# A graph attention layer on one core: 66 tiles of gathered node rows filled by ScalarE from a transposed table

## The chip, the cores and the metric

The kernel runs on one core of a Trainium2 chip. The metric is the device time of one execution in microseconds (us). The core has five engines with instruction queues of their own: TensorE (PE; its weight loads are shown as PEld), VectorE (DVE), ScalarE (ACT), GpSimd (POOL) and SyncE (SP), and 16 DMA engines that all of them share. A DMA that SyncE or ScalarE issues has one fixed pattern of addresses; GpSimd issues the indirect DMAs, in which each row's address comes from a list of indices.

## The reference, cut to what matters

N = 12500 nodes and E = 200000 edges, 64 features, 2 heads, all in 32-bit floats. The edges are sorted by `dst`; `src` is random.

```python
h = maximum(_layernorm(x), 0)
h_edge = ((h[src] + bond) @ W).reshape(-1, H, D)
el = einsum('ehd,hd->eh', h_edge, attn_l)
er = einsum('nhd,hd->nh', (h @ W).reshape(-1, H, D), attn_r)
s = leaky_relu(el + er[dst], 0.2)
ex = exp(s - segment_max(s, dst)[dst])
alpha = ex / segment_sum(ex, dst)[dst]
ft = segment_sum(h_edge * alpha[..., None], dst).mean(axis=1)
out = x + relu((ft - ft.mean(0)) / sqrt(ft.var(0) + eps) * gamma + beta)
```

## The kernel before, in words

The edges are cut into 49 chunks of 4096 (`NCH`), a chunk into 16 groups g of 256 edges, a group into two tiles j of 128 edges, one edge a partition. So a chunk has 32 tiles (j, g), the last chunk 27. A quarter k of a chunk is four groups, 8 tiles.

**h.** At the start VectorE and ScalarE normalise x into h (125 partitions, 100 nodes each). TensorE turns h in 13 rounds of up to four blocks (`er_table`, line 803) and ScalarE copies each round from PSUM (`evacuate`, line 667) for the node scores. Each row of h with its two source scores, 66 floats, is written to the table `h_tab` in HBM (line 482). Chunks 0 and 1 gather rows of x instead and are normalised on the fly.

**The gathers.** GpSimd fetches each tile with one indirect DMA (`gather`, line 592; issue at line 599): 128 rows of `h_tab` at the indices in `srcI`, into the buffer `gat` of the chunk (two of them, in turn). `tiles_of(c, k)` lists the tiles of a quarter. Before some gathers GpSimd waits: for VectorE to have used the buffer's quarter two chunks ago (`e_ok`), and by `keep_step_late` (line 582), from chunk 5 on, at the chunk's gather 1 for the sums of two chunks before and at its gather 17 for the turned weights of the chunk before (`p_turned`). In chunks 2 to 4 `keep_step` has such waits of its own, among them chunk 3's `p_turned` at gather 27 of chunk 4.

**SyncE's tiles.** In 21 chunks (`SP_TILES`, 6, 8, ... 46) the last tile (1, 15) isn't gathered. SyncE fetches its 128 rows one by one into `sp_tile` (`load_rows`, line 484): it loads 16 offsets into registers (line 391) and issues 16 DMAs of one row each (line 491), and so on, 64 rows a chunk. In between it loads the chunk's destination numbers (`load_dst`) and the next chunk's bond features (`load_bond`, 1024 KB). For this VectorE turned the numbers of nodes into offsets at the start (line 1207, `offs_ok`).

**A chunk's work** (`chunk(c)` on each engine). For each quarter TensorE turns the bond features into PSUM bank `pt` (`turn`, line 833) and VectorE's `make_e` (line 1047) copies the two scores of each row to `elh` (line 1055) and adds h and bond into `edge` (line 1060). In a quarter with a tile of SyncE's it does that in three pieces each. TensorE adds up the scores of a chunk in PSUM `sT_ps` (32 rows, head by group, of 256 edges): `bond_scores` from the bond features (line 851), `near_scores` for the destinations (line 871), `far_scores` from `elh` (line 879). ScalarE copies them to `s_raw` (line 730), VectorE applies the leaky relu (line 1289) and finds the segments' maxima, ScalarE makes `fexp` (line 736) and `pT` (line 740), TensorE turns `pT` into `p_m` (line 926, `p_turned`), VectorE scales the one-hot matrix (line 1342), TensorE makes the sums (line 942) and VectorE adds them to `acc`, [65, 2, 12532], at columns that are read from registers (line 1370). The nodes that are finished are turned to z in blocks of 250 (`z_block`, `z_turn`), which ScalarE keeps in the space of `acc` (`z_keep`, line 720) and VectorE puts into the statistics. After the last chunk come the batch norm, ScalarE's scaling (line 776), TensorE's turning back, and the output.

Each engine runs its queue in order, with semaphores written out by hand. VectorE's `step` waits for each operation's end before the next.

## Time and profile before

| | |
|---|---|
| runs | 1986.5, 1991.77, 1992.52 us; median 1991.77 |
| profiled execution, span from first to last instruction | 1992.0 us |
| busy share | GpSimd 74%, VectorE 55%, TensorE 48%, ScalarE 6% |
| gathers of h | 1478 |
| single-row DMAs of SyncE | 2688 |
| granted TensorE clock, mean | 0.663 |

The page names no other time of the profiled execution than its span, which lies within 0.3 us of the runs' median. A busy share is an average over the span. Register loads and the issue of DMAs on SyncE and ScalarE aren't counted as busy; GpSimd's indirect DMAs are, for as long as it makes their descriptors. "issue" as the end of an idle time says that the engine waited for nothing that the profile shows. For each line of the chain of waits the profile follows back what released it.

### The profile page before, as it was taken

How to read it: one execution, taken by the hardware profiler on the slowest of the kernel's cores; microseconds unless marked ns; L12 is line 12 of the kernel's file. 1: busy time of each engine (PE TensorE's matmuls, PEld its weight loads, DVE VectorE, ACT ScalarE, POOL GpSimd, SP SyncE). 2: the span in 40 equal slices, each digit the busy share in tenths (PEclk: the TensorE clock that was granted, in tenths of full speed). 3: DMA queues.
4: the chain of work that ended last, by engine and by line, in shares of the span. 5: the costliest groups of instructions: out<-in, count | busy, mean ns of one | idle time of the engine just before them, and what ended most of it. 6: DMA issues, size and time to landing. Idle time of an engine off the chain costs nothing.

```text
span 1992.0 us, 24940 instructions
## 1 busy us (share of the span) xinstructions
PE 958.3 (48%) x6252; PEld 731.4 (37%) x6252; DVE 1094.0 (55%) x3217; ACT 120.8 (6%) x243; POOL 1474.7 (74%) x1559
## 2 busy tenths in 40 slices
PE   2647544543554435345534453554454444544455
PEld 2525333432343324234323342343234333433345
DVE  7888545544654545446545454555465545544555
ACT  2420000000000000000000000000000000000002
POOL 7777777777777777777777777777777777777771
PEclk9867766666666666666666676667666766666677
DMA  7333222223222322232223222322322222223215
GB/s 205 93 92 93 61 71 82 61 61 92 60 61 61 91 62 61 61 92 61 60 66 85 62 61 60 92 61 61 87 65 61 60 70 83 60 61 93 60 39 135
DMA packets 75938, 149.57 MB, mean 75 GB/s; under 512 B 33559, under 2 KB 36465, under 8 KB 69265
## 3 DMA queue, kind: packets, MB, share of 16 engines
q0 software_dynamic: 49568, 52.34, 14.3%
q1 hardware_dynamic: 25106, 91.83, 13.3%
q10 hardware_dynamic: 1112, 3.73, 0.7%
q8 instruction: 52, 0.85, 0.2%
q14 instruction: 100, 0.81, 0.1%
HBM read 141.18 MB, written 6.60 MB: 74 GB/s over the span
## 4 chain that ended last, share of the span: by engine, by line
POOL 71%; issue 23%; PE 2%; DVE 2%; DMA 1%; ACT 0%; ACTq 0%; SPq 0%; DVEq 0%; POOLq 0%
POOL work L599 71%; PE p_s L821 1%; PE pt L810 0%; DMA h_tab<-acc 0%; DMA acc<-in_x 0%; DVE acc L1101 0%; DVE acc L1099 0%; POOL er_run L613 0%; PE po L942 0%; PE pt L994 0%; DVE acc L1108 0%; DMA work<-h_tab,srcI 0%; PE po L994 0%; DVE work L1085 0%; PE p_r L994 0%
## 5 line engine op out<-in xcount | busy, mean ns | idle before, releaser
L599 POOL DMA_INDIRECT work<-h_tab,srcI x1478 | 1403.9, 950 | 451.1 <-issue 451.1
L1055 DVE COPY elh<-work 128x16 f32<-128x16 f32 (+2 forms) x217 | 40.7, 196 | 761.2 <-DMA work<-h_tab,srcI 760.9
L879 PE MATMUL p_s<-ident,elh 128*32 128x128 f32 x196 | 50.6, 412 | 615.7 <-DVE elh L1055 615.7
L942 PE MATMUL po<-scaled,work 128*65 128x64 f32 x3104 | 292.5, 281 | 61.6 <-issue 58.6
L942 PEld LDWEIGHTS po<-scaled,work 128*65 128x65 f32 x3104 | 287.1, 198 | 79.5 <-issue 78.6
L879 PEld LDWEIGHTS p_s<-ident,elh 128*32 128x32 f32 x196 | 25.9, 155 | 641.4 <-DVE elh L1055 637.1
L842 PE MATMUL pt<-ident,work 128*128 128x128 f32 x784 | 187.0, 386 | 73.9 <-DVE work L1060 73.8
L851 PE MATMUL p_s<-work,wpair 128*32 128x256 f32 x784 | 183.2, 388 | 1.6 <-DVEq L1016 1.6
L1370 DVE TENSOR_TENSOR acc<-acc,po 65x64 f32 x776 | 168.5, 217 | 27.6 <-DVE acc L1370 1.4
L842 PEld LDWEIGHTS pt<-ident,work 128*128 128x128 f32 x784 | 137.8, 207 | 83.8 <-DVE work L1060 81.9
L1060 DVE TENSOR_TENSOR work<-work,pt 128x512 f32<-128x512 f32 (+2 forms) x217 | 133.1, 621 | 0.4 <-PE pt L842 0.3
L851 PEld LDWEIGHTS p_s<-work,wpair 128*32 128x32 f32 x784 | 83.7, 112 | 86.1 <-issue 13.9
L1342 DVE TENSOR_TENSOR scaled<-onehot,p_m 128x2048 f32<-128x2048 f32 x48 | 109.6, 2284 | 5.2 <-PE p_m L926 5.2
L730 ACT ACTIVATE s_raw<-p_s 32x256 f32<-32x256 f32 x49 | 18.3, 374 | 1427.1 <-PE p_s L879 1427.1
L871 PE MATMUL p_s<-ohT_i,er_st 128*32 128x256 f32 x392 | 94.3, 384 | 7.1 <-DVE er_st L1203 7.1
L793 PEld LDWEIGHTS p_q<-wz,acc 65*125 65x125 f32 x376 | 83.2, 324 | 0.2 <-issue 0.2
L793 PE MATMUL p_q<-wz,acc 65*125 65x65 f32 x376 | 82.5, 398 | 0.0
L599 POOL DMA_INDIRECT work<-in_x,srcI x64 | 63.0, 984 | 20.8 <-issue 18.9
L926 PE MATMUL p_m<-ident,pT 32*128 32x32 f32 x98 | 20.4, 300 | 95.6 <-ACT pT L740 95.6
L923 PE MATMUL p_m<-fexp,ones 1*65 1x2 f32 x98 | 18.2, 252 | 91.4 <-ACT fexp L736 91.4
L871 PEld LDWEIGHTS p_s<-ohT_i,er_st 128*32 128x32 f32 x392 | 43.5, 111 | 49.3 <-DVE er_st L1203 7.2
L1201 DVE TENSOR_TENSOR ohT_i<-ohT_i,p_m 128x1024 f32<-128x1024 int32 x49 | 59.5, 1215 | 1.9 <-DMA ohT_i<-in_dst_n 1.9
(194 smaller groups left out, 962.2 us busy)
## 6 DMA issues: line engine op xcount, KB each, us to landing
work<-in_ea_t SPq DMA_DIRECT2D x49, 1024.0 KB, 7.4
sp_tile<-h_tab SPq DMA_DIRECT2D x2688, 0.3 KB
ohT_i<-in_dst_n SPq DMA_DIRECT2D x49, 512.0 KB
work<-h_tab,srcI POOLq DMA_INDIRECT x1478, 2.4
h_tab<-acc SPq DMA_DIRECT2D x1, 2887.5 KB
work<-in_x SPq DMA_DIRECT2D x1, 2800.0 KB
out<-work SPq DMA_DIRECT2D x5, 448.0 KB
acc<-in_x ACTq DMA_DIRECT2D x3, 672.0 KB
```

Of the source, the lines that this page charges most:

```text
L599: pool.indirect_dma_start(out=row, out_offset=None, in_=x if c < RAW else h_tab, in_offset=bass.IndirectOffsetOnAxis(ap=srcI[:, c, j, g:g ...
L793: m = mm(z_bank(b)[0:NP_, c0:c0 + F1], view(acc[0:F1, hd, 0:1], [[NR, NP_]], b * ZBL + r), wz[:, hd, :], start=True, stop=True)
L842: m = nc.tensor.transpose(pt[n % 2][:, (j * 2 + i) * P:(j * 2 + i + 1) * P], bt[c % 2][:, 2 * k + i, j * P:(j + 1) * P], ident[:, :])
L851: m = mm(sT_ps, wpair[:, i, :, :].rearrange("p h g -> p (h g)"), bt[c % 2][:, i, :], start=(i == 0), stop=False, skip_group_check=True)
L871: m = mm(sT_ps, er_st[:, b, :, :].rearrange("p h g -> p (h g)"), ohT[:, b, :], start=False, stop=False, skip_group_check=True)
L879: m = mm(sT_ps[:, j * P:(j + 1) * P], elh[:, c % 2, j, :, :].rearrange("p h g -> p (h g)"), ident[:, :], start=False, stop=True, skip_grou ...
L942: m = mm(bank[0:F1, w0:w0 + H * WIN], edge[c % 2][:, j, g, :], scaled[:, j * CG + g, :, :].rearrange("p h w -> p (h w)"), start=(j == 0), ...
L1055: copied = v.tensor_copy(elh[:, q, js, :, g0:g1], rows_h[:, :, :, F:FH].rearrange("p j g h -> p j h g"))
L1060: added = v.tensor_tensor(edge[q][:, js, g0:g1, 0:F], rows_h[:, :, :, 0:F], turned[:, js, g0 - GQ * k:g1 - GQ * k, :], ALU.add)
L1201: also(v.tensor_tensor(ohT, ohT_i[:, :, :], view(tgt[:, c * NB4:(c + 1) * NB4], [[1, NB4], [0, GROUP]]), ALU.is_equal))
L1342: v.tensor_tensor(scaled[:, :, :, :], view(onehot[:, :, :], [[WIN, CT], [0, H], [1, WIN]]), view(p_m[:, 0:H * CT], [[1, CT], [CT, H], [0, ...
L1370: added = v.tensor_tensor(at, at, bank[0:F1, w0:w0 + H * WIN].rearrange("p (h w) -> p h w", h=H), ALU.add)
```

## The change

1. **66 tiles are filled by ScalarE.** `col_tiles(c)`: from chunk 5 on the tile (0, 12), in even chunks (1, 12) too. `tiles_of` leaves them out, in all 66 gathers that GpSimd doesn't issue. In their place in `gat` zeros are written once.
2. **A transposed h.** The 13 rounds of turned h, which ScalarE already copies from PSUM, are also written to a table `hT_tab` [64, 12500] in HBM by 26 DMAs. After `h_tab` is written SyncE reads it back into partitions 96 to 127 of `acc`, where both halves of `acc` had nothing after the start: 32 features in each half (`hT_cols`). The rounds are kept in four buffers instead of two. VectorE turns the node numbers into columns of that table (`coffs`, ten operations). ScalarE's first chunk waits for both.
3. **The copies.** After a chunk's `pT`, ScalarE runs `load_cols(c)`: 6 batches, each of which loads 32 column numbers into registers and copies 32 columns of 32x2 numbers into `cols`.
4. **TensorE adds them** with the identity as weights into `pt` on top of the turned bond features (`turn`, for k = 3), and with `col_w` into the scores (`bond_scores`).
5. **No single-row transfers.** SyncE's `load_rows`, `sp_tile`, `offs` are gone; `make_e` has one copy and one addition again.
6. **Scores from PSUM.** ScalarE's copy to `s_raw` is gone; VectorE multiplies `sT_ps` by 0.2 into `s_low` and takes the larger of the two.
7. **z.** As partitions 96 to 127 are taken, z blocks 0 to 44 are kept in two halves in partitions 0 to 63, and one DMA puts them together at the end (`z_packed`). Some small tiles share space, and the reserve for the descriptors of GpSimd's DMAs is set to 4096 bytes a partition (`dynamic_dma_scratch_size`).

```diff
+def col_tiles(c):
+    if c < COL_FIRST:
+        return []
+    return [(j, COL_G) for j in range(EPP if c % 2 == 0 else 1)]
...
                     if (c * CG + g) * GROUP + j * P < E
-                    and not (c in SP_TILES and (j, g) == (EPP - 1, CG - 1))]
+                    and (j, g) not in col_tiles(c)]
...
+            for n, (i0, i1) in enumerate(HT):
+                sp.wait_ge(hT_ok, n + 1)
+                for b in range(EPP):
+                    sp.dma_start(hT_tab[:, b * NH + i0 * NP_:b * NH + i1 * NP_].rearrange("f (i p) -> f i p", p=NP_),
+                                 hT(n)[b * F:(b + 1) * F, 0:i1 - i0, :]).then_inc(hT_out[n % 4], 16)
...
+            sp.wait_ge(lent_free, 1)
             sp.wait_ge(htab_in, 32)
+            sp.wait_ge(ertab_in, 48)
+            for i in range(4):
+                sp.wait_ge(hT_out[i], 32 * len(HT[i::4]))
+            for i in range(H):
+                sp.dma_start(hT_cols[:, i, :], hT_tab[i * HALF:(i + 1) * HALF, :]).then_inc(cols_table_in, 16)
             for c in range(1, NCH):
-                n, half = divmod(c - (SP_TILES[0] - SP_LEAD), SP_LEAD)
-                if 0 <= n < len(SP_TILES):
-                    sp.wait_ge(sums_made, 2 * (c - 1))
-                    load_rows(n, 2 * half)
                 load_dst(c)
                 if c + 1 < NCH:
                     load_bond(c + 1)
-                if 0 <= n < len(SP_TILES):
-                    sp.wait_ge(p_turned, c)
-                    load_rows(n, 2 * half + 1)
+            sp.wait_ge(zT_ok, Z_IN)
+            sp.dma_start(zT[F:P, 0:Z_IN, :], view(acc[0:F, 1, :], [[NP_, Z_IN], [1, NP_]])).then_inc(z_packed, 16)
...
+            def load_cols(c):
+                b0 = COL_BATCHES * (c - COL_FIRST + 2)
+                for cc, j, r0 in col_batches[b0:b0 + COL_BATCHES]:
+                    n = cols_upto(cc - 1) + j
+                    if n >= COL_BUFS:
+                        act.wait_ge(cols_read, n - COL_BUFS + 1)
+                    for i, r in enumerate(col_regs(cc, j * P + r0, j * P + r0 + COL_BATCH), r0):
+                        copied = nc.scalar.activation(view(cols[0:HALF, n % COL_BUFS, 0, i:i + 1], [[P, H]]),
+                                                      view(acc[CP:P, 0, bass.ds(r, 1)], [[NACC, H]]), ACT.Copy)
+                    copied.then_inc(cols_ok, 1)
...
-                act.wait_ge(scores_made, c + 1)
-                nc.scalar.activation(s_raw[:, :], sT_ps, ACT.Copy).then_inc(scores_ok, 1)
...
                 nc.scalar.activation(pT[:, :], sdif[:, :], ACT.Exp).then_inc(p_ok, 1)
+                if COL_FIRST - 2 <= c < NCH - 2:
+                    load_cols(c)
...
+            act.wait_ge(coffs_ok, 1)
+            act.wait_ge(cols_table_in, 32)
...
+                dve.wait_ge(scores_made, c + 1)
+                step(v.tensor_scalar(s_low[:, :], sT_ps, NEG_SLOPE, None, ALU.mult))
+                v.tensor_tensor(sL, sT_ps, s_low[:, :], ALU.max).then_inc(scores_ok, 1)
                 dve.wait_ge(scores_ok, c + 1)
-                step(v.scalar_tensor_tensor(sL, s_raw[:, :], NEG_SLOPE, s_raw[:, :], ALU.mult, ALU.max))
...
-    nc = _bacc.Bacc("TRN2", target_bir_lowering=False, num_devices=1)
+    nc = _bacc.Bacc("TRN2", target_bir_lowering=False, num_devices=1, dynamic_dma_scratch_size=4096)
```

How the instructions stand in the queues, at three places. Each row is a line of the kernel, an operation, what it writes and reads, and what it waits for.

ScalarE before, from the middle of one chunk into the next (`s_raw` are the copied scores, `acc` from `p_q` a kept z block):

```order
L736 ACTIVATE fexp<-fdif 1x2 [waits open_all,open_diff]
L740 ACTIVATE pT<-sdif 32x256 [waits p_turned,diff_ok]
L730 ACTIVATE s_raw<-p_s 32x256 [waits scores_made]
L723 ACTIVATE acc<-p_q 128x125 [waits zT_made]
L736 ACTIVATE fexp<-fdif 1x2 [waits open_all,open_diff]
```

ScalarE now, chunk 3, the first with copies. A batch is one TENSOR_LOAD (32 registers) and 32 times the pair of ISA (the register instruction that makes the address) and ACTIVATE:

```order
L753 ACTIVATE acc<-p_q 64x125 [waits zT_made]
L753 ACTIVATE acc<-p_q 64x125
L783 ACTIVATE fexp<-fdif 1x2 [waits open_all,open_diff]
L787 ACTIVATE pT<-sdif 32x256 [waits p_turned,diff_ok]
L418 TENSOR_LOAD coffs
L767 ISA
L767 ACTIVATE cols<-acc 32x2
```

In every chunk from 3 to 46 there are now 6 such batches, 391 instructions more, between `pT` and the next chunk's z block and `fexp`; the wait for the scores is gone from this queue.

GpSimd before, its whole run of gathers of h:

```order
L613 DMA er_run<-er_tab,er_idx 16x64
L599 DMA work<-h_tab,srcI 128x66 x1478
L404 TENSOR_LOAD flag
```

and now:

```order
L636 DMA er_run<-er_tab,er_idx 16x64
L622 DMA work<-h_tab,srcI 128x66 x1433
L429 TENSOR_LOAD flag
```

There are 45 fewer, and the order is the same.

TensorE before, from a chunk's sums to the wait for the gathered rows' scores:

```order
L942 MATMUL po<-scaled,work 65x64 x15
L842 MATMUL pt<-ident,work 128x128 [waits e_ok]
L842 MATMUL pt<-ident,work 128x128 x3
L851 MATMUL p_s<-work,wpair 32x256 [waits scores_ok]
L851 MATMUL p_s<-work,wpair 32x256 x7
L871 MATMUL p_s<-ohT_i,er_st 32x256 [waits near_ok]
L871 MATMUL p_s<-ohT_i,er_st 32x256 x3
L879 MATMUL p_s<-ident,elh 32x128 [waits elh_ok]
```

and now, in the same place, ahead of an odd chunk (one tile):

```order
L1007 MATMUL po<-scaled,work 65x64 x15
L897 MATMUL pt<-ident,work 128x128 [waits cols_ok,e_ok]
L900 MATMUL pt<-ident,cols 128x32 x2
L897 MATMUL pt<-ident,work 128x128 x3
L910 MATMUL p_s<-work,wpair 32x256 [waits scores_ok]
L910 MATMUL p_s<-work,wpair 32x256 x7
L915 MATMUL p_s<-cols,col_w 32x128 x2
L936 MATMUL p_s<-ohT_i,er_st 32x256 [waits near_ok]
L936 MATMUL p_s<-ohT_i,er_st 32x256 x3
L944 MATMUL p_s<-ident,elh 32x128 [waits elh_ok]
```

Four multiplications more a tile, and a wait for the copied columns, both ahead of the wait for `elh`.

## Rows read from the trace of the kernel before

**Rows 1.** Page: busy us (share) xinstructions of each engine; chain that ended last, by engine

```profile
PE 958.3 (48%) x6252; PEld 731.4 (37%) x6252; DVE 1094.0 (55%) x3217; ACT 120.8 (6%) x243; POOL 1474.7 (74%) x1559
...
POOL 71%; issue 23%; PE 2%; DVE 2%; DMA 1%; ACT 0%; ACTq 0%; SPq 0%; DVEq 0%; POOLq 0%
```

**Rows 2.** Page, costliest groups: line engine op xcount | busy, mean ns | idle before

```profile
L599 POOL DMA_INDIRECT work<-h_tab,srcI x1478 | 1403.9, 950 | 451.1 <-issue 451.1
```

**Rows 3.** Waits of GpSimd: waited for, us in total, times, longest us

```profile
POOL work L599 <- issue: 470.0, 1540, 0.3
```

**Rows 4.** Timeline of GpSimd: start us, us, engine line op, idle before; four gathers

```profile
94.87 0.96 POOL L599 DMA_INDIRECT work<-h_tab,srcI  x1 [0.30 <-issue]
...
208.87 0.95 POOL L599 DMA_INDIRECT work<-h_tab,srcI  x1 [0.31 <-issue]
...
355.62 0.94 POOL L599 DMA_INDIRECT work<-h_tab,srcI  x1 [0.30 <-issue]
...
1948.63 0.95 POOL L599 DMA_INDIRECT work<-h_tab,srcI  x1 [0.30 <-issue]
```

**Rows 5.** Waits of VectorE and of TensorE, the longest of each

```profile
DVE elh L1055 <- DMA work<-h_tab,srcI: 760.9, 159, 12.2
...
PE p_s L879 <- DVE elh L1055: 615.7, 45, 18.1
```

**Rows 6.** Timeline of ScalarE at the start, three neighbours

```profile
41.43 0.59 ACT L673 ACTIVATE onehot<-pt 128x500 f32<-128x500 f32 x1 [2.39 <-PE pt L810]
41.91 0.21 ACT L665 ACTIVATE acc<-acc 125x24 f32<-125x24 f32 x1
42.03 1.48 ACT L678 ACTIVATE acc<-acc 125x1536 f32<-125x1536 f32 x1
```

**Rows 7.** Timeline of VectorE, eight additions to acc

```profile
319.33 1.98 DVE L1370 TENSOR_TENSOR acc<-acc,po 65x64 f32 x8
```

**Rows 8.** Timeline of SyncE's queue, two groups of 16 transfers; tile sp_tile, its issues

```profile
194.52 5.12 SPq L491 DMA_DIRECT2D sp_tile<-h_tab  x16
...
201.01 5.09 SPq L491 DMA_DIRECT2D sp_tile<-h_tab  x16
...
L491 SPq DMA_DIRECT2D sp_tile<-h_tab x2688: 224/228/329, 179.8 to 1821.3; - x192
```

**Rows 9.** Timeline of ScalarE, one chunk's two exponentials

```profile
302.58 0.20 ACT L736 ACTIVATE fexp<-fdif 1x2 f32<-1x2 f32 x1 [4.40 <-DVEq L1016]
...
304.69 0.42 ACT L740 ACTIVATE pT<-sdif 32x256 f32<-32x256 f32 x1 [1.90 <-DVE sdif L1318]
```

**Rows 10.** Timeline of TensorE, the turned weights of a chunk

```profile
348.77 0.42 PE L926 MATMUL p_m<-ident,pT 32*128 32x32 f32 x2 [1.94 <-ACT pT L740]
```

**Rows 11.** Windows (engines' busy us, clock, DMA share, GB/s); timeline of VectorE

```profile
334.00:336.00 2.00, 0.00 (x0) 0.00 (x0) 0.00 (x0) 0.00 (x0) 1.39 (x3) 0.50 0.94 377
...
339.12 0.17 DVE L1055 COPY elh<-work 128x16 f32<-128x16 f32 x1 [10.95 <-DMA work<-h_tab,srcI]
```

**Rows 12.** Windows at the start; VectorE and ScalarE there; page, DMA issues (us to landing)

```profile
40.00:60.00 20.00, 20.00 (x101) 20.00 (x101) 17.88 (x28) 9.14 (x13) 15.31 (x16) 1.00 0.12 26
...
72.00:84.00 12.00, 7.61 (x31) 4.56 (x30) 11.80 (x13) 7.07 (x2) 8.95 (x11) 0.92 0.92 293
...
84.97 0.22 DVE L1207 TENSOR_SCALAR offs<-offs 48x128 int32<-48x128 int32 x1
...
124.13 0.20 ACT L736 ACTIVATE fexp<-fdif 1x2 f32<-1x2 f32 x1 [4.41 <-DVEq L1016]
...
work<-in_ea_t SPq DMA_DIRECT2D x49, 1024.0 KB, 7.4
```

**Rows 13.** Timeline of TensorE, the turned weights of chunk 3

```profile
191.59 0.42 PE L926 MATMUL p_m<-ident,pT 32*128 32x32 f32 x2 [1.95 <-ACT pT L740]
```

**Rows 14.** Timeline of ScalarE at the end, the first of its last scalings

```profile
1974.34 3.21 ACT L776 ACTIVATE acc<-acc,col 128x250 f32<-128x250 f32 x4 [0.75 <-DVE col L1483]
```

**Rows 15.** Page, DMA issues: the gathers, median us from issue to landing

```profile
work<-h_tab,srcI POOLq DMA_INDIRECT x1478, 2.4
```

More of the change, by code:

```diff
@@ L50, with cols_upto @@
 PRE = NZ - 6
-SP_LEAD = 2
-SP_TILES = range(6, NCH - 1, SP_LEAD)
-SP_PARTS = (0, 32, 64, 96, 128)
-BATCH = 16
+NH = N // EPP
+COL_G = 12
+COL_FIRST = 5
+COL_BUFS = 4
+COL_BATCH = 32
+COL_BATCHES = 6
+def col_tiles(c):
+    if c < COL_FIRST:
+        return []
+    return [(j, COL_G) for j in range(EPP if c % 2 == 0 else 1)]
+def cols_upto(c):
+    return sum(len(col_tiles(i)) for i in range(c + 1))
 ZIN = NZ - 1
@@ L108, in gnn_kernel @@
         elh = sb("elh", [P, 2, EPP, H, CG])
-        offs = sb("offs", [P, P], i32)
-        sp_tile = sb("sp_tile", [P, 2, FH])
+        coffs, coffs_t, coffs_u = (sb(n, [P, EPP * P], i32) for n in ("coffs", "coffs_t", "coffs_u"))
+        cols = sb("cols", [P, COL_BUFS, H, P])
+        col_w = sb("col_w", [P, H, H, CG])
         raw_mv = sb("raw_mv", [P, 2, EPP, CG])
@@ L264, in gnn_kernel @@
         ertab_in = sem("ertab_in")
-        offs_in = sem("offs_in")
-        offs_ok = sem("offs_ok")
-        sp_rows_in = [sem(f"sp_rows_in{i}") for i in range(4)]
+        coffs_in = sem("coffs_in")
+        coffs_ok = sem("coffs_ok")
+        hT_out = [sem(f"hT_out{i}") for i in range(4)]
+        cols_table_in = sem("cols_table_in")
+        cols_ok = sem("cols_ok")
+        cols_read = sem("cols_read")
+        z_packed = sem("z_packed")
         er_idx_in = sem("er_idx_in")
@@ L386, in tiles_of, with col_regs @@
                     if (c * CG + g) * GROUP + j * P < E
-                    and not (c in SP_TILES and (j, g) == (EPP - 1, CG - 1))]
-        def far_regs(c, o0, o1, last, which):
+                    and (j, g) not in col_tiles(c)]
+        def col_regs(c, o0, o1):
             return nc.values_load_multi_w_load_instructions(
-                offs[c:c + 1, o0:o1], engines=[which], min_val=0, max_val=last,
+                coffs[c:c + 1, o0:o1], engines=[mybir.EngineType.Activation], min_val=0, max_val=N - 1,
                 skip_runtime_bounds_check_because="src and dst hold numbers of nodes")[1]
-        h_bytes = h_tab.rearrange("n f -> (n f)").bitcast(u8)
         def gathers_upto(c, k):
@@ L723, in z_keep, with z_keep_halves @@
                 nc.scalar.activation(zT[:, b, :], z_turned(b), ACT.Copy).then_inc(kept, 1)
+            def z_keep_halves(b):
+                act.wait_ge(zT_made, b + 1)
+                for r in range(NR):
+                    kept = nc.scalar.activation(acc[0:F, r, b * NP_:(b + 1) * NP_], z_turned(b)[r * F:(r + 1) * F], ACT.Copy)
+                kept.then_inc(zT_ok, 1)
+            col_batches = [(c, j, r0) for c in range(NCH) for j, g in col_tiles(c) for r0 in range(0, P, COL_BATCH)]
+            assert len(col_batches) <= COL_BATCHES * (NCH - COL_FIRST)
+            def load_cols(c):
[8 more added lines that the diff above has]
+                    copied.then_inc(cols_ok, 1)
             def chunk(c):
@@ L728, in chunk @@
                     z_keep(NZ - 5, zT_made, zT_ok)
[L729 to L732 removed]
+                if c == NCH - 1:
+                    z_keep(NZ - 4, zT_made, zT_ok)
+                else:
+                    for b in z_seen(c):
+                        z_keep_halves(b)
                 act.wait_ge(open_diff, c + 1)
@@ L853, in bond_scores @@
                 m.then_inc(bond_scored, 1)
+                for j, g in col_tiles(c):
+                    for i in range(H):
+                        m = mm(sT_ps[:, j * P:(j + 1) * P], col_w[0:HALF, i, :, :].rearrange("p h g -> p (h g)"),
+                               cols[0:HALF, (cols_upto(c - 1) + j) % COL_BUFS, i, :], start=False, stop=False,
+                               skip_group_check=True)
+                    m.then_inc(cols_read, 1)
             def own_turn():
@@ L1131, in _ @@
             step(v.tensor_copy(wB[:, :, :], view(wlr[0:F, :], [[1, H], [0, P]])))
+            for i in range(H):
+                step(v.tensor_copy(col_w[0:HALF, i, :, COL_G], wlr[i * HALF:(i + 1) * HALF, 0:H]))
             signal(wr_ok)
@@ L1261, in z_stat, with z_stat_halves @@
                 also(v.bn_stats(stats[:, at:at + BN6], zT[:, b, :]))
+            def z_stat_halves(b):
+                dve.wait_ge(zT_ok, b + 1)
+                at = b * BN6 + (3 if b >= PRE else 0)
+                for r in range(NR):
+                    also(v.bn_stats(stats[r * F:(r + 1) * F, at:at + BN6], acc[0:F, r, b * NP_:(b + 1) * NP_]))
             def pre_stats():
@@ L1392, in closing @@
                 v.bn_stats(stats[:, (NZ - 1) * BN6 + 3:NZ * BN6 + 3], z_turned(NZ - 1)).then_inc(last_read, 1)
+            for i in range(2):
+                dve.wait_ge(hT_out[i], 32 * len(HT[i::4]))
             for c in range(NCH - 2):
```

105 lines of the change are left out of this document (58 added, 47 removed).

## The prediction

> **What bounds the kernel now.** I read the page's busy shares first, then the chain of waits, then GpSimd's row and its waits, and then one period of the timeline engine by engine. GpSimd is busy 74% of the span, more than any other engine, and 71% of the chain that ended last is its own [rows 1]. That is its line 599, the indirect gather: 1403.9 us of work and 451.1 us of "issue" gaps for 1478 gathers, so (1403.9 + 451.1) / 1478 = 1.255 us each [rows 2]. Its waits show nothing but "issue", 0.3 us at the longest, so GpSimd never waits for a result [rows 3]; it goes on from the first gather of h (94.87 us) to the last one (1948.63 us), and a tail of 43.4 us follows [rows 4]. The others wait for it: VectorE 760.9 us for gathered rows, TensorE 615.7 us for VectorE behind them [rows 5]. So the time is the count of gathers times 1.255 us, plus start and tail, as long as no other engine needs more than a period. A period is one chunk: before, 31 gathers in the 21 chunks in which SyncE helps, 32 in the others.
>
> **What the change takes from GpSimd.** Of the 66 tiles that ScalarE now fills, 21 take the place of tiles that SyncE fetched row by row. The gathers of h fall from 1478 to 1433, and 45 x 1.255 = 56.5 us, all on the chain.
>
> **What it costs ScalarE.** This is the unknown. Between two chunks' exponentials ScalarE now runs 6 batches, each a load of 32 registers and 32 pairs of a register instruction and a copy of 32x2 numbers.
> *A pair.* From below: on ScalarE an operation with 24 elements a partition starts at 41.91 and the next at 42.03, though it takes 0.21; so 0.12 us apart; 500 elements take 0.59, that is (0.59 - 0.21) / 476 = 0.8 ns an element, so with 2 instead of 24 it would be 0.10 [rows 6]. From above: VectorE's line 1370 is such a pair, and 8 take 1.98 us, 0.25 each; but there each operation awaits the end of the one before, and the register instruction is hidden under it [rows 7]. In between: 16 of SyncE's row transfers, each behind one register move, take 5.12 us, so 0.32 each, of which the transfer's issue is 0.228; a register instruction with its gaps is worth 0.09 on a queue [rows 8]. A pair is then the longer of 0.10 (engine) and 0.09 plus a short hand-over (queue). I take 0.105 us, nearest to ScalarE's own row, and keep 0.10 and 0.25 as ends.
> *A load.* SyncE loads 16 registers between two groups of 16 transfers: 201.01 - 194.52 - 5.12 = 1.37 us [rows 8]. For 32 that is between 1.4 (all of it fixed) and 2.7 (all by the register); I take the middle, 2.1.
> *A chunk.* Six loads 12.6; 192 pairs 20.2; from the start of fexp to the end of pT 304.69 + 0.42 - 302.58 = 2.5 [rows 9]; a z block kept in two halves, twice some 0.25, 0.5. Sum 35.8 us. The period becomes 30 or 31 gathers in turn, 30.5 x 1.255 = 38.3 us. So ScalarE fits, with 2.5 us to spare; a pair of (38.3 - 12.6 - 3.0) / 192 = 0.118 us is where it no longer does.
> Queued behind the copies on ScalarE is the next chunk's fexp and pT; TensorE waits for those (p_m), VectorE's scaled one-hot for TensorE, the sums for VectorE. GpSimd, too, waits at its gather 17 for the p_m of the chunk before: turned at 348.77 + 0.42 = 349.19, reached at 355.62, 6.4 us of slack [rows 4, 10]. So a single late exponential costs nothing, only an average above the period does.
> The Trainium skill ("ScalarE: Activation LUTs", What ACT_TABLE_LOAD costs) gives an ACTIVATE with immediate operands 186 ns + 0.833 ns an element, with about 93 ns of overlap between neighbours; an estimate from it is 0.095 us a copy, and a chunk would be 33.8. The trace agrees as far as its operations go; none of its rows has a copy behind a register instruction.
>
> **SyncE** loses 2688 row transfers of 0.32 us, 20 us a chunk and more. They were hidden, but held up the loads behind them (1.5 MB a chunk), which then met the last gathers: from 334 to 336 us the DMA engines are 94% busy, and that chunk's last rows are used at 339.12 only, after 10.95 us of waiting [rows 11]. That collision goes and brings nothing, since GpSimd doesn't wait for it.
> **VectorE** loses some small copies and additions in every second chunk, and gains one operation of about 0.4 us on the scores (it reads them from PSUM where ScalarE copied them first). It is 55% busy; I cost this at nothing, under its 760.9 us of waiting [rows 1, 5]. In the last chunk that cover is gone: 0.3 us.
> **TensorE** gets four short multiplies a tile, up to 3 us a chunk, under 615.7 us of waiting in 45 places, 13.7 each [rows 5]. Nothing.
>
> **The start.** VectorE gets ten operations on 49x256 numbers ahead of chunk 0. One on 48x128 takes 0.22, so ten are about 4 us: fexp of chunk 0 moves from 124.13 to 128.5. ScalarE also has to wait there for the turned table: written in 26 pieces from 38 us on, while the DMA engines are 12% busy, and read back, 3.2 MB, after the flag at about 88. At the 293 GB/s of 72 to 84 us that takes 11 us, at the pace of a 1024 KB load in 7.4 us it takes 23: it lands at 99 to 111, ahead of 124 [rows 12]. The h table's own write (72 to 84) keeps its place before GpSimd's first gather of it. What is late next is GpSimd's gather 27 of chunk 4 at 208.87, which needs the p_m of chunk 3, turned at 191.59 + 0.42; 17 us of slack take the 4 [rows 4, 13]. Nothing.
> **The end.** One DMA of 1.4 MB packs the z blocks of all but the last chunks. It isn't wanted before ScalarE's last scaling at 1974.34, and takes 5 to 10 us at the two paces above [rows 12, 14]. Nothing.
>
> **Sum.** The profiled execution spans 1992.0 us, 0.2 above the median of the runs, 1991.8. 1991.8 - 56.5 + 0.3 = **1935.6 us**.
>
> **The rivals.** *A. ScalarE becomes the bound.* The chain then runs over its 44 stretches of copies. Each 0.01 us of a pair above 0.118 costs 192 x 0.01 x 44 = 84 us, less 6.4 of slack once. At 0.13 the period is 12.6 + 25.0 + 3.0 = 40.6: 44 x 2.3 - 7 = 94 over the forecast, **2030 us**. At the upper end, 0.25, it would be over 3000. For it: the margin is 2.5 us in 38, and no row has the pair. Against it: 0.12 with 24 elements on the engine itself. It decides from a pair of 0.118, or a load of 2.5. Chance 0.16.
> *B. A little of that:* a pair of 0.119 to 0.125 (at 0.121 the period is 38.8, 44 x 0.5 - 7 = 15 more), or the column table comes tens of us late and the first chunks with it. **1941 to 1985 us**. Chance 0.08.
> *C. Gathers get dearer.* The reserve for their descriptors is set to 4096 bytes. A gather lands 2.4 us after its issue and the next follows after 1.255, so two are under way [rows 2, 15]. If the reserve held only one, each would cost 2.4 in place of 1.255: 1433 x 1.15 = 1650 us more, **3580 us**. No row shows how many it holds. Chance 0.01.
> *D. Register loads are slow.* At 0.2 us a register a load is 6.4, a chunk 38.4 + 20.2 + 3.0 = 61.6, and the time 1935.6 + 44 x 23.3 - 7 = **2954 us**. Rows 8 speak against it, 16 registers in 1.37. Chance 0.02. The figure of 0.2 is the Trainium skill's ("Runtime: NRT & Kernel Launch", Instruction fetch mechanics); the trace doesn't agree for SyncE's loads, 0.086 at most.
> *E. No change:* a pair near 0.126 gives back what was won, 1986 to 1998. Chance 0.03.
>
> **How the numbers follow.** The forecast has 0.70. About 0.3%, 6 us, is what a measurement of this kernel can tell from no change. Faster: 0.70 + 0.08 = 0.78; within 0.3%: 0.03; slower: 0.16 + 0.01 + 0.02 = 0.19. The range takes the forecast and B, and the edge of E: 1929 (the spread of the runs, 6 us, below) to 1988. The forecast's own is 1929 to 1941.
>
> **What would show it.** Right: 1433 gathers at 1.255 us with "issue" gaps alone, the last one near 1892; 8448 copies in stretches of about 33 us, with ScalarE idle between a stretch and the next fexp; the column table landed before 120 us. Wrong: GpSimd waiting for TensorE's p_m; ScalarE without idle time in mid-kernel; periods over 38.3 us. "Issue" gaps over 0.3 us on GpSimd would speak for C.

## The result, and the profile after

The changed kernel takes 1943.2 us (median of 4 runs, 1941.2 to 1946.5) against 1992.1 for the kernel before on the same chip (4 runs, 1986.5 to 1992.9): ratio 0.9759, 95% interval 0.9744 to 0.9775, so 2.4% faster. The forecast was 1935.6, with 1929 to 1941 as its own range and 1929 to 1988 as the whole one. The sign, the mechanism and the size are right; the time came out 7.6 us above the forecast, 2 us outside its own range. The profiled execution spans 1941.6 us.

The page of the changed kernel (busy us and share; the chain that ended last; the two groups that matter, with busy us, mean ns of one and the idle time before them):

```profile
PE 1074.3 (55%) x6780; PEld 791.7 (41%) x6780; DVE 1130.0 (58%) x3242; ACT 1053.2 (54%) x8687; POOL 1426.6 (73%) x1514
...
POOL 63%; issue 22%; DVE 7%; PE 4%; DMA 1%; ACT 1%; ACTq 1%; DVEq 0%
...
L622 POOL DMA_INDIRECT work<-h_tab,srcI x1433 | 1356.3, 946 | 444.1 <-issue 436.7
L767 ACT ACTIVATE cols<-acc 32x2 f32 x8448 | 939.0, 201 | 524.8 <-issue 503.3
```

Beside [rows 1, 2] ScalarE has gone from 6% busy to 54%, and has only 1% of the chain, its queue another 1%. GpSimd has 1433 gathers instead of 1478, but its idle time is no longer all "issue": 444.1 - 436.7 = 7.4 us have another cause. Its waits, and those of the engines that feed it, name that cause (engine line waited for: us in total, times, longest):

```profile
PE p_q L845 <- ACT acc L753: 145.2, 43, 18.3
PE p_m L988 <- ACT fexp L783: 31.9, 14, 12.7
DVE scaled L1419 <- PE p_m L991: 26.5, 28, 13.8
ACT L783 <- DVEq L1081: 25.9, 1, 25.9
PE po L928 <- DMA er_run<-er_tab,er_idx: 21.8, 1, 21.8
...
POOL work L622 <- PE p_m L991: 7.4, 1, 7.4
```

GpSimd waits once, 7.4 us, for p_m, the turned weights of a chunk; before there was no such line [rows 3]. The timeline of ScalarE shows from where (start us, us, engine line op, count, idle before):

```profile
138.22 1.28 ACT L783 ACT_TABLE_LOAD   x1 [25.86 <-DVEq L1081]
139.52 0.20 ACT L783 ACTIVATE fexp<-fdif 1x2 f32<-1x2 f32 x1
...
202.81 0.20 ACT L783 ACTIVATE fexp<-fdif 1x2 f32<-1x2 f32 x1 [3.44 <-DVEq L1081]
204.92 0.41 ACT L787 ACTIVATE pT<-sdif 32x256 f32<-32x256 f32 x1 [1.91 <-DVE sdif L1395]
207.23 3.51 ACT L767 ACTIVATE cols<-acc 32x2 f32 x32 [1.90 <-issue]
212.66 2.66 ACT L767 ACTIVATE cols<-acc 32x2 f32 x24 [1.91 <-issue]
...
237.50 1.16 ACT L767 ACTIVATE cols<-acc 32x2 f32 x10 [0.18 <-issue]
238.69 0.55 ACT L753 ACTIVATE acc<-p_q 64x125 f32<-64x125 f32 x2
239.27 0.20 ACT L783 ACTIVATE fexp<-fdif 1x2 f32<-1x2 f32 x1
239.38 0.40 ACT L787 ACTIVATE pT<-sdif 32x256 f32<-32x256 f32 x1
```

and that of GpSimd:

```profile
234.69 0.95 POOL L622 DMA_INDIRECT work<-h_tab,srcI  x1 [0.31 <-issue]
243.00 0.95 POOL L622 DMA_INDIRECT work<-h_tab,srcI  x1 [7.36 <-PE p_m L991]
...
1893.53 0.95 POOL L622 DMA_INDIRECT work<-h_tab,srcI  x1 [0.31 <-issue]
```

Chunk 0's fexp comes at 139.52 instead of 124.13 [rows 12], so chunk 3's comes at 202.81; the first stretch of copies, 33.3 us long, runs from 205.3 to 238.66; chunk 4's exponentials stand behind it; and GpSimd, at gather 17 of chunk 5, has to wait for them until 243.0. After that it never waits again. The last gather starts at 1893.53, 55.1 us earlier than before [rows 4]. The tail after it is 1941.6 - 1893.5 = 48.1 us instead of 43.4. So 45 gathers and some shorter gathers won about 62 us, the one wait cost 7.1 (7.4 less the gap of 0.3), and the tail 4.7.

### The profile page after: what moved, and what is told of

Same layout as the page of the kernel before. It is cut to its first block, busy times and chain, and to the rows that moved or that the text cites. A ratio compares the mean times of both kernels' runs of the same rounds, so it can differ in the third digit from the quotient of the medians.

```text
span 1941.6 us, 37629 instructions
## 1 busy us (share of the span) xinstructions
PE 1074.3 (55%) x6780; PEld 791.7 (41%) x6780; DVE 1130.0 (58%) x3242; ACT 1053.2 (54%) x8687; POOL 1426.6 (73%) x1514
## 4 chain that ended last, share of the span: by engine, by line
POOL 63%; issue 22%; DVE 7%; PE 4%; DMA 1%; ACT 1%; ACTq 1%; DVEq 0%
POOL work L622 63%; PE p_s L873 1%; PE po L1007 1%; DMA acc<-in_x 1%; ACT cols L767 1%; ACTq L418 1%; PE pt L862 1%; DVE work L1148 0%; DVE scaled L1146 0%; DMA work<-h_tab,srcI 0%; DVE acc L1447 0%; PE p_s L910 0%; PE pt L897 0%; DVE acc L1156 0%; DVE acc L1154 0%
## 5 line engine op out<-in xcount | busy, mean ns | idle before, releaser
L622 POOL DMA_INDIRECT work<-h_tab,srcI x1433 | 1356.3, 946 | 444.1 <-issue 436.7
L767 ACT ACTIVATE cols<-acc 32x2 f32 x8448 | 939.0, 201 | 524.8 <-issue 503.3
L1108 DVE COPY elh<-work 128x16 f32<-128x16 f32 x196 | 37.7, 193 | 638.1 <-DMA work<-h_tab,srcI 636.5
L1007 PE MATMUL po<-scaled,work 128*65 128x64 f32 x3104 | 289.5, 280 | 63.9 <-issue 60.9
L1007 PEld LDWEIGHTS po<-scaled,work 128*65 128x65 f32 x3104 | 284.2, 196 | 81.7 <-issue 80.9
L944 PE MATMUL p_s<-ident,elh 128*32 128x128 f32 x196 | 49.8, 406 | 409.4 <-DVE elh L1108 409.4
L897 PE MATMUL pt<-ident,work 128*128 128x128 f32 x784 | 203.5, 393 | 60.5 <-DVE work L1112 60.0
L910 PE MATMUL p_s<-work,wpair 128*32 128x256 f32 x784 | 202.4, 417 | 1.6 <-DVEq L1081 1.6
L944 PEld LDWEIGHTS p_s<-ident,elh 128*32 128x32 f32 x196 | 25.7, 154 | 434.6 <-DVE elh L1108 430.1
L1112 DVE TENSOR_TENSOR work<-work,pt 128x512 f32<-128x512 f32 x196 | 132.9, 678 | 1.0 <-PE pt L897 0.9
L910 PEld LDWEIGHTS p_s<-work,wpair 128*32 128x32 f32 x784 | 89.9, 120 | 98.9 <-issue 34.6
L783 ACT ACTIVATE fexp<-fdif 1x2 f32<-1x2 f32 x49 | 9.9, 203 | 119.8 <-DVEq L1081 119.6
L787 ACT ACTIVATE pT<-sdif 32x256 f32<-32x256 f32 x49 | 20.3, 415 | 85.7 <-DVE sdif L1395 85.7
L1252 DVE TENSOR_TENSOR onehot<-p_m,rel_i 128x1024 f32<-128x1024 f32 x49 | 59.6, 1217 | 0.2 <-DVE coffs L1308 0.2
## 6 DMA issues: line engine op xcount, KB each, us to landing
acc<-hT_tab SPq DMA_DIRECT2D x2, 1562.5 KB, 14.2
```

What stands on the lines that cost most here:

```text
L622: pool.indirect_dma_start(out=row, out_offset=None, in_=x if c < RAW else h_tab, in_offset=bass.IndirectOffsetOnAxis(ap=srcI[:, c, j, g:g ...
L767: copied = nc.scalar.activation(view(cols[0:HALF, n % COL_BUFS, 0, i:i + 1], [[P, H]]), view(acc[CP:P, 0, bass.ds(r, 1)], [[NACC, H]]), AC ...
L897: m = nc.tensor.transpose(pt[n % 2][:, at:at + P], bt[c % 2][:, 2 * k + i, j * P:(j + 1) * P], ident[:, :])
L910: m = mm(sT_ps, wpair[:, i, :, :].rearrange("p h g -> p (h g)"), bt[c % 2][:, i, :], start=(i == 0), stop=False, skip_group_check=True)
L944: m = mm(sT_ps[:, j * P:(j + 1) * P], elh[:, c % 2, j, :, :].rearrange("p h g -> p (h g)"), ident[:, :], start=False, stop=True, skip_grou ...
L1007: m = mm(bank[0:F1, w0:w0 + H * WIN], edge[c % 2][:, j, g, :], scaled[:, j * CG + g, :, :].rearrange("p h w -> p (h w)"), start=(j == 0), ...
```

## The experiments

On two of the five visits to a chip that these runs took, the first two, the kernel before took about 2624 us instead of 1988 to 1992, and each variant that also ran on a normal visit was slower too. They are told last, because they need the others to be read. The changed kernel itself, run again as a control on a normal visit:

> The changed kernel as it is, a control. In the last two calls the kernel before took 2623 to 2625 us where it had taken 1992, and its relatives lost time to engines waiting for their next instruction. Theory A (a condition of those visits, in which instructions reach the engines slowly, and which weighs on straight-line code with very many short instructions): if the kernel before takes about 2624 here, the changed kernel takes 3040 to 3080, since late_numbers and tail_full, which are almost it, did. If before takes about 1992, this one takes 1943. Theory B (the slow times come from the edits of those kernels): the changed kernel takes less than before here too, ratio about 0.976.

It took 1938.7 us against 1988.0 (ratio 0.9751, 0.9735 to 0.9767), theory A's case. It has the same wait at the same gather (7.5 us after 233.95), the last gather at 1889.9, span 1937.7. The other kernels of normal visits are compared with this one.

**Start, stall and tail: late_both.**

```
-    if c < COL_FIRST:
+    if c < COL_FIRST or c == NCH - 1:            # no column tiles in the last chunk
...
+            sp.wait_ge(own_turned, 1)            # SyncE, ahead of the column table's load
             for i in range(H):
                 sp.dma_start(hT_cols[:, i, :], ...)
...
+                if b0 == 0:                      # ScalarE, in load_cols
+                    act.wait_ge(coffs_ok, 1)
+                    act.wait_ge(cols_table_in, 32)
...
-            act.wait_ge(coffs_ok, 1)             # ScalarE, ahead of chunk 0
-            act.wait_ge(cols_table_in, 32)
...
                 chunk(c)
+                if c == 0:                       # VectorE: the ten operations on coffs
+                    col_numbers()
```

> The changed kernel with three edits whose effects stand in different places of the trace: column numbers and ScalarE's waits moved behind chunk 0; column table loaded after er_run is turned; no column tiles in the last chunk (two gathers more, 1435). Theory: the start is back (fexp(0) at about 125 instead of 139.5), so GpSimd's one wait of 7.1 us goes; the last gather starts at 1893.5 - 7.1 + 2.5 = 1889.0 and the tail behind it is back from 48.1 to about 43.5. Time 1938.7 (the changed kernel in the last call) - 7.1 + 2.5 - 4.6 = about 1929.5. Rival 1 (the first stretch of copies makes the stall by itself): stall stays 7, time 1936.6. Rival 2 (the tail is long for a cause in the end phase): tail stays 48, time 1934. If the slow condition of the first calls is back, only the order of the traces is read.

Measured 1931.6 us (ratio 0.9712, 0.9698 to 0.9725), 7.1 us less than the changed kernel where 9.2 were expected. Its timelines of ScalarE, TensorE (start), GpSimd (last gather) and TensorE (end):

```profile
125.48 0.20 ACT L787 ACTIVATE fexp<-fdif 1x2 f32<-1x2 f32 x1 [14.09 <-DVEq L1083]
...
95.56 2.00 PE L930 MATMUL po<-ident,er_run 128*32 128x32 f32 x112 [10.21 <-DMA er_run<-er_tab,er_idx]
...
1887.17 0.94 POOL L623 DMA_INDIRECT work<-h_tab,srcI  x1 [0.30 <-issue]
...
1882.35 1.89 PE L938 MATMUL p_s<-ohT_i,er_st 128*32 128x256 f32 x8
1884.56 1.14 PE L847 MATMUL po<-wz,acc 65*125 65x65 f32 x8 [0.32 <-issue]
...
1890.21 1.06 PE L946 MATMUL p_s<-ident,elh 128*32 128x128 f32 x4 [4.39 <-DVE elh L1110]
```

Three things are to be seen. *The start:* fexp of chunk 0 is at 125.48, and the wait for p_m has gone from GpSimd's list altogether. er_run, VectorE's input for chunk 0, is turned at 95.56. In the changed kernel that row is

```profile
109.68 2.09 PE L928 MATMUL po<-ident,er_run 128*32 128x32 f32 x112 [21.78 <-DMA er_run<-er_tab,er_idx]
```

14 us later, because the seven gathers of er_run landed beside the column table's own load, whose two DMAs of 1562.5 KB were issued at 91.01 and took 14.2 us each; from 91 to 110 us the DMA engines are 96% busy, against 13% from 88 to 97 in late_both, where the table's load comes at 97.9. The other runs bear it out: the row stands at 95.8 to 96.5 in the kernel before, b_scratch, b_no_rows_2 and all_in, which have no such load there, and at 107.5 to 109.7 in the four normal executions that have it. VectorE had other work for part of that and stood for 5.9 us, until 0.1 us after TensorE had turned er_run (109.68 + 2.09 = 111.77):

```profile
103.67 2.29 DVE L1140 SCALAR_TENSOR_TENSOR work<-work,p_q 128x2048 f32<-128x2048 f32 x1
111.88 0.56 DVE L1284 COPY er_all<-po 128x384 f32<-128x384 f32 x1 [5.93 <-issue]
...
127.64 0.36 DVE L1299 TENSOR_SCALAR coffs_t<-coffs 49x256 int32<-49x256 int32 x1
...
132.07 1.23 DVE L1252 TENSOR_TENSOR onehot<-p_m,rel_i 128x1024 f32<-128x1024 f32 x1 [0.21 <-DVE coffs L1308]
```

The 15.4 us of delay are then 5.9 for er_run; 4.4 for the ten operations (127.64 to 132.07); 1.3 for the load of the Exp table, which used to lie in idle time and now stood right ahead of fexp; 3.2 by which VectorE's row at 103.67 was late already (it stood at 100.43 before, at 101.40 in late_both); and 0.6 of small shifts. Of the 3.2, late_both shows 1.0 as well; the other 2.2 were there at 83 us already, before the table's load was issued, and their cause is open. *The stall:* rival 1, that the first stretch makes it by itself, falls. *The tail:* 1930.7 - 1887.2 = 43.5 us. The rows of the changed kernel at that place:

```profile
1891.42 3.64 PE L910 MATMUL p_s<-work,wpair 128*32 128x256 f32 x16
1894.99 1.06 PE L915 MATMUL p_s<-cols,col_w 32*32 32x128 f32 x8
1895.98 1.91 PE L936 MATMUL p_s<-ohT_i,er_st 128*32 128x256 f32 x8
1899.85 1.14 PE L845 MATMUL po<-wz,acc 65*125 65x65 f32 x8 [1.95 <-issue]
...
1901.04 0.71 PE L944 MATMUL p_s<-ident,elh 128*32 128x128 f32 x4
```

There TensorE adds the last gathered scores (L944) 7.5 us after the last gather; in late_both (L946) 3.0 us after it, and there it waits for VectorE, which waits for the gather. In the changed kernel it waits for nothing but its own list: the sums of chunk 47, the column multiplies, a z block. That list starts when chunk 47's last gather is in, and the last chunk, two gathers shorter, no longer covers it. Two gathers more, 2.5 us, made the tail 4.6 us shorter. Rival 2 falls. The tail also shortens with the tiles taken out of the last chunk: 48.1 us with two, 44.6 with one (one_tile_2, below), 43.5 with none; two_tiles, with two as well, has 45.4, but there ScalarE and not GpSimd sets the pace. The 2 us that are missing in the time lie in the gathers, as far as the two profiled executions tell: their mean is 946.9 ns here and 945.4 in after_again, over 1506 of them 2.3 us. Why is not shown.

Not separated: the three start edits went in together here, so how much of the stall each would have taken is not shown.

**The value of a gather, and the break point: one_tile_2 and two_tiles.** Edit of the first: `range(EPP if c % 2 == 0 else 1)` becomes `range(1)` and COL_BATCHES 4; of the second: `range(EPP)` and 8.

> One column tile in every chunk (44 tiles), 22 gathers more than the changed kernel, in the condition in which that takes 1938.7. Theory: 22 x 1.252 = 27.5 more, no stall (7.1 less) as a stretch takes 22.2 us, tail about 2 less: about 1957. Rival (ScalarE's copies cost each period something beside the gathers): under 1953.

Measured 1955.8 us (ratio 0.9839, 0.9825 to 0.9852), no wait on GpSimd, tail 1956.1 - 1911.5 = 44.6. From one_tile_2 to late_both 20 gathers fewer and 24.2 us less, the shorter tail (1.1 us) included. So ScalarE's 2560 copies more (8192 against 5632) cost next to nothing: the rival falls. It bears on the stall too: chunk 0's fexp is late here as well (137.5), but the first stretch is four batches instead of six, and GpSimd doesn't wait. So the stall took both, the late start and the long stretch.

```profile
L622 POOL DMA_INDIRECT work<-h_tab,srcI x1455 | 1375.1, 945 | 443.3 <-issue 442.7
```

> Two column tiles in every chunk (88 tiles, eight batches), 22 gathers fewer (1411). By the gathers alone it would be 27.5 us faster, about 1911. Theory: ScalarE then needs 8 x 5.55 = 44.4 us of copies, and some 3 to 4 us of other work and waits at each chunk's turn, against a period of 30 gathers or 37.5 us, so it sets the pace: 43 stretches of about 48 us, 2064 us, on a start of 203 us and a tail of some 70: about 2330, 17 per cent slower than before. Rival (copies overlap the register loads or the pace of gathers holds): 1911 to 1950.

Measured 2246.6 us (ratio 1.1299, 1.1282 to 1.1316): 22 gathers fewer than in the change, and 13% slower than before. Its waits, and one turn of ScalarE between stretches:

```profile
PE p_q L845 <- ACT acc L753: 920.5, 45, 29.3
...
POOL work L622 <- PE p_m L991: 355.0, 44, 16.9
```

```profile
1009.69 3.30 ACT L767 ACTIVATE cols<-acc 32x2 f32 x30 [1.97 <-issue]
1013.17 0.31 ACT L767 ACTIVATE cols<-acc 32x2 f32 x2 [0.18 <-issue]
1013.50 0.55 ACT L753 ACTIVATE acc<-p_q 64x125 f32<-64x125 f32 x2
1014.08 0.20 ACT L783 ACTIVATE fexp<-fdif 1x2 f32<-1x2 f32 x1
1014.19 0.40 ACT L787 ACTIVATE pT<-sdif 32x256 f32<-32x256 f32 x1
1015.68 3.51 ACT L767 ACTIVATE cols<-acc 32x2 f32 x32 [1.09 <-issue]
```

GpSimd now waits in every chunk, and ScalarE, in the turn shown, for nothing but its register loads: a stretch, the z halves, the two exponentials and the next stretch stand end to end. This is the prediction's rival A, made on purpose. The mechanism is as expected, the size was not: I had 48 us a chunk, and it is 44.9 on average, 45.2 from the turn shown to the next, since at the bound all that ScalarE needs is ready and the turn costs 1.1 us and a gap of 1.1 instead of 3 to 4. A batch is 5.40 to 5.80 us, 5.6 on average. An estimate from these rows: with six batches instead of eight ScalarE would need 45.2 - 2 x 5.6 = 34.0 us a chunk, against 30.5 x 1.25 = 38.1 of gathers: the change has 4 us to spare, more than the 2.5 of the prediction.

**The single rows put back: all_in.** It is late_both plus SyncE's 21 single-row tiles as in the kernel before, except that their offsets and rows lie in coffs_u and coffs_t:

```
+        sp_tile = view(coffs_t[:, :], [[FH, 2], [1, FH]]).bitcast(f32)
+        offs = coffs_u[:, 0:P]
...
+                    and not (c in SP_TILES and (j, g) == (EPP - 1, CG - 1))]
...
+                    sp.wait_ge(sums_made, 2 * (c - 1))
+                    load_rows(n, 2 * half)
```

> late_both with SyncE's 21 single-row tiles put back (rows of tile (1, 15) of every second chunk, as in the kernel before): 1414 gathers. Theory: 21 x 1.252 = 26.3 us less than late_both, given back some 5 us as gathers last over 1000 ns again beside the row transfers, and an even chunk then has 28 gathers or 35.1 us against ScalarE's 35.8 at most every second chunk, whose average with the odd ones (30 gathers, 37.6 us) still covers it: 1929.5 - 26.3 + 5 = about 1908. Rival (ScalarE and SyncE late in the short chunks): stalls of 1 to 3 us in each pair of chunks, 1930 to 1990.

Measured 1904.9 us (1903.3 to 1905.2), ratio 0.9578, 0.9565 to 0.9591: 1.8% less by the ratios than the change, 4.2% less than before, the best of all. (The expectation miscounted the gathers of a chunk: they are 29 and 31, 30 on average.) 26.6 us less than late_both for 21 gathers, 1.27 each; nothing is given back, 11 gathers are over 1000 ns, GpSimd has no wait over 0.3 us once it gathers rows of h, and the tail is 43.4.

```profile
L664 POOL DMA_INDIRECT work<-h_tab,srcI x1414 | 1335.2, 944 | 431.2 <-issue 430.9
```

**The kernel before with one part of the change: b_scratch and b_no_rows_2.** The first has dynamic_dma_scratch_size=4096; the second has SP_TILES empty, with the two calls of load_rows taken out.

> The kernel before with the descriptor reserve of the change (4096) and nothing else. The rival of the prediction that a small reserve stalls GpSimd's gathers expects them far slower; the theory expects no stall. Still open is why 49 gathers of the kernel before last over 1000 ns (some 5.4 us in all) and 8 to 11 in the changed kernel and in all_in, which has SyncE's row transfers too. Theory A (the larger reserve, together with the row transfers): few such gathers here, time about 1988 - 5 = 1983. Theory B (not the reserve): 40 to 50 of them, time as before, 1988.

1987.8 us against 1987.2, ratio 1.0003, 0.9994 to 1.0012: the reserve costs and brings nothing, so rival C of the prediction falls. The time is theory B's; the count of gathers over 1000 ns, 29, lies between the two theories.

> The kernel before without SyncE's row transfers (1499 gathers), in the condition in which the kernel before takes 1988. A gather is worth 1.252 us, so 21 of them 26.3. Theory A (the long gathers need the row transfers in the kernel before, as the 4 long ones of the slow visit say): under 15 of them, time 1988 + 26.3 - 5 = about 2009. Theory B (the slow visit hid them): some 45 of them, time about 2014.

2013.4 us, ratio 1.0129, 1.0113 to 1.0144: 26.2 us for 21 gathers, 1.25 each. But 44 gathers are long, so here theory A falls and B's time fits: without the row transfers there are 44, about as many as the 49 before, so those don't make them long, and the larger reserve alone does not bring them down to the count of the change. Counted over all traces of normal visits, gathers longer than 1000 ns are 49, 29 and 44 in the kernel before and these two, and 6 to 11 in the six executions with a column table. What in the change does it is open. It is worth little: the excess of all gathers over their median is 6.7, 6.0 and 6.2 us in the three, and 1.2 to 3.9 in the others.

**The slow visits.** Four kernels went to one chip and one to another, and on both the kernel before took 2623 to 2625 us. It was the visit and not the chip: b_scratch and b_no_rows_2 ran later on the first of them, late_both, one_tile_2, two_tiles and all_in on the second, and the kernel before took 1987.2 and 1988.4 us there. late_numbers is late_both's edits of VectorE and ScalarE alone; late_table adds the one of SyncE; tail_full is the last-chunk edit alone; one_tile and b_no_rows are as above.

> The changed kernel, with VectorE's computing of the column numbers moved behind chunk 0 and ScalarE's two waits (numbers, column table) moved to its first copies. Theory: the one wait of GpSimd (7.1 us lost at gather 17 of chunk 5) comes from a late start: fexp(0) was 15.4 us late, of which VectorE's 10 rows are 4.6 and the Exp table load right before it 1.3. fexp(0) comes at about 133.6 instead of 139.5, the stall shrinks to about 1.2 us, last gather about 1887.7, time about 1937.3. Rival (the first stretch of copies alone makes the stall, whenever the chunks start): stall still 7, time 1943.

> As late_numbers, and SyncE loads the column table only once er_run is turned. Theory: the rest of the late start (about 9 us) is er_run's seven gathers, which land late beside the 3 MB table load. fexp(0) comes at about 125, no stall, last gather about 1886.5, time about 1936.1: little under late_numbers, as only 1.2 us of stall were left. Rival (er_run lands late for another cause): fexp(0) stays at 133 to 134, stall about 1, time as late_numbers.

> The changed kernel without column tiles in the last chunk: two gathers more (1435). Theory: the tail grew from 43.4 to 48.1 us because TensorE's work from chunk 47's end on takes a fixed time, and the last chunk became two gathers (2.5 us) shorter and 2.3 us of multiplies longer. Last gather 2.5 us later (1896.0), tail back to about 43.5, time 1943.2 - 2.3 = about 1941: not slower though it gathers more. Rival (the tail is longer for a cause in the end phase itself): tail stays 48, time 1945.7.

> The changed kernel with one column tile in every chunk (44 tiles, four batches in a stretch), 22 gathers more (1455). Theory: a gather is worth 1.25 us, a stretch of copies takes 22.2 us instead of 33.3, so no stall: last gather 1893.5 + 27.5 - 7.1 = 1914.0, tail about 46, time about 1961. Rival (ScalarE's copies slow each period by something): the 22 gathers cost less than 27.5 - 7.1 = 20.4 us more, time under 1957.

> The kernel before without SyncE's 21 single-row tiles: GpSimd gathers them, 1499 gathers of h_tab in place of 1478. Theory A (SyncE's row transfers are what makes 49 gathers of the kernel before last over 1000 ns, 5.4 us in all; the changed kernel has 8 such): 21 x 1.25 = 26.3 us more, less about 5, time about 1992 + 21 = 2013, and under 15 gathers over 1000 ns. Theory B (those gathers are long for another cause, ScalarE's or the descriptor space's): time about 2018, and still some 45 gathers over 1000 ns. If the chip is again in the condition of the last call, where the kernel before took 2625 us and all engines waited for their next instructions, the count of long gathers still decides.

Measured: late_numbers 3079.4 (ratio 1.1731, 1.1712 to 1.1750), late_table 3076.9 (1.1718, 1.1698 to 1.1738), tail_full 3041.8 (1.1593, 1.1568 to 1.1618), one_tile 2660.1 (1.0133, 1.0116 to 1.0150), b_no_rows 2346.1 (0.8942, 0.8924 to 0.8960). None of the expected times came out. b_no_rows has 4 gathers over 1000 ns, which reads like its theory A; but the same kernel has 44 on a normal visit (b_no_rows_2), so the count decided nothing here. In tail_full the page's row of the copies, the longest waits, and ScalarE in one stretch are:

```profile
L767 ACT ACTIVATE cols<-acc 32x2 f32 x8192 | 1048.0, 203 | 1575.7 <-issue 1574.7
```

```profile
ACT cols L767 <- issue: 1574.7, 1741, 3.3
...
POOL work L622 <- PE p_m L991: 912.0, 47, 25.0
...
PE po L1007 <- issue: 581.0, 368, 2.6
```

```profile
1003.37 3.51 ACT L767 ACTIVATE cols<-acc 32x2 f32 x32 [1.07 <-issue]
1008.82 1.81 ACT L767 ACTIVATE cols<-acc 32x2 f32 x16 [1.94 <-issue]
1011.52 0.31 ACT L767 ACTIVATE cols<-acc 32x2 f32 x2 [0.89 <-issue]
...
1014.10 0.21 ACT L767 ACTIVATE cols<-acc 32x2 f32 x1 [1.13 <-issue]
```

A copy still takes 203 ns and the first 48 of this stretch keep their pace; then ScalarE stands for half a microsecond or more after every one or two, without a releaser. late_both, with as many copies, has 372 gaps before them, 495.2 us, its register loads above all; here there are 1741. What grows is the register instruction ahead of a copy (FUSED_REGOPS in the trace), first in tail_full and then in late_both (times each; shortest, median, longest ns; first and last start us):

```profile
L767 ACTq FUSED_REGOPS  x8192: 3/46/1409, 265.5 to 2933.9; - x200
...
L771 ACTq FUSED_REGOPS  x8192: 46/46/57, 198.2 to 1811.6; - x200
```

TensorE has such gaps too, between its sums (L1007), where there is no register instruction. A gather still takes 947 ns. So what is late is not data. The loss on a slow visit, the last column of the table, rises with the number of instructions that the trace has, but not in proportion: 6638 more of them, from the kernel before to one_tile, raise it by 68 us, and 5500 more, from there to tail_full, by 406.

| kernel | instructions | slow visit, us | normal visit, us | difference |
|---|---|---|---|---|
| b_no_rows | 19,293 | 2346 | 2013 | 333 |
| kernel before | 24,940 | 2624 | 1988 | 636 |
| one_tile | 31,578 | 2660 | 1956 | 704 |
| tail_full (normal: late_both, as many) | 37,078 | 3042 | 1932 | 1110 |

A reading that fits is that instructions reached the engines slowly on those visits. It is argued and not shown: the page's row of the instruction queue has 185 packets and 1.52 MB in tail_full as in late_both, with 0.2% and 0.3% of the DMA engines' time, so those transfers took no longer. A count of instructions alone doesn't make a kernel slow either: two_tiles has 43,680 and all_in 42,729, both on a normal visit. What the chips were doing then is not shown, nor was the changed kernel itself run there; late_numbers, which differs from it only in where two waits and ten operations stand, was 17% slower than the kernel before. What these runs can decide beside that is the tail: 3042.5 - 2999.3 = 43.2 us in tail_full, 3073.2 - 3026.2 = 47.0 in late_numbers and 3085.7 - 3040.4 = 45.3 in late_table, which both keep the column tiles in their last chunk. The last-chunk edit alone brings the tail back, and the start edits alone do not. The stall the variants of the change can't decide, since GpSimd waits in nearly every chunk there (46 or 47 times for p_m).

## Why the prediction was right, and where it missed

**What bounds the kernel: right.** GpSimd's gathers set the pace before and after, at the trace's own pitch of 1.251 us each, and three differences of whole kernels lie round it: 26.2 us for 21 (b_no_rows_2, 1.25 each), 26.6 for 21 (all_in, 1.27), 24.2 for 20 (one_tile_2 to late_both, 1.21). The 56.5 us of the first term are 56.3 by that pitch.

**ScalarE fits under the gathers: right.** A pair was taken at 0.105 us and is 0.107; a load of 32 registers at 2.1 and is 1.99 on average, about 2.1 with the gaps round it:

```profile
L418 ACTq TENSOR_LOAD <-coffs x264: 1947/1978/2171, 204.9 to 1865.0; - x132
```

Six batches were 32.8 and are 33.4. The step counts two exponentials at 2.5 us, which at the bound take less; the margin, by the estimate from two_tiles, is 4 us and not 2.5. two_tiles shows that the break point is real and what lies behind it. Rival D falls by the same row: 1.99 us for 32 registers is 0.062 each. The Trainium skill's 0.2 us a register ("Runtime: NRT & Kernel Launch", Instruction fetch mechanics) does not hold for these loads from SBUF.

**The start: mis-sized, and with it the step that says nothing stalls.** "fexp of chunk 0 moves from 124.13 to 128.5" was the ten operations alone, and they did take 4.4 us. Missing were the gathers of er_run, held up by the 3.2 MB table load (5.9 us of standing VectorE), the Exp table load right ahead of fexp (1.3), and some 3 us by which VectorE was late before: 139.5. I had asked whether the load would land in time for ScalarE, which it did (about 105), and not what else was landing then. And the slack was checked for the one chunk before the first stretch (17 us, enough for 15), but not for the chunk after it, where the delay and the first stretch of 33 us add up. There it cost 7.1 us.

**The tail: mis-sized.** "The end ... Nothing" and "0.3 us" looked at the packing DMA and VectorE's extra operation. The tail grew by 4.7 us, since two of the 45 gathers came out of the last chunk, under whose gathers TensorE's work for the chunk before was hidden. Those two were worth less than nothing.

**Not in the prediction: a gain.** Fewer long gathers, some 5 us in the profiled pair of executions, cause open. The balance of the profiled executions: 1992.0 - 56.3 - 5.5 + 7.1 + 4.7 = 1942.0, against 1941.6. That the time came out as near as 7.6 us is in part luck: the two terms left out cost 11.8 us, and this gain, which no step foresaw, took off about half of it.

**The rivals.** A was the one to fear, and is one tile a pair of chunks away; B's range (1941 to 1985) is where the time fell, but by neither of its conditions: a pair is 0.107 us and the table landed at about 105. The first chunks were late, as in its second branch, through er_run and VectorE's own work; C and D fall; E did not come. On the slow visits something decided that was on nobody's list, and it is still open.

## What to carry to other kernels

Where one engine's count of operations sets the time, price the operation once and then look for what the change does to the ends: work hidden under the last operations of the bound engine comes out when these are taken away, so take them from the middle. A large transfer that lands in time for its own reader can still make a small one beside it late; ask what else is on the DMA engines at that moment. And before idle time of an engine is filled with thousands of tiny instructions, compare the gain (2.4% here) with what visits like those two can take (late_numbers, all but the changed kernel, was 17% slower than the kernel before there). That of two ways to the same gain the one with fewer instructions is the safer is a guess from those visits, not shown.
